# A graph network on one core: SP fetches seven tiles by rows instead of five, with their indices read five at a time, and the two padding tiles are not gathered

## What is computed

```python
edge_index = jnp.stack([src, dst])
h = jnp.maximum(_layernorm(x, axis=-1), 0.0)
x = x + _L0_gnn_ref(h, src, dst, L0_gnn_weight, L0_gnn_b)             # mean of h[src] (and self), times W
h = jnp.maximum(_layernorm(x, axis=-1), 0.0)
x = x + _L1_gnn_ref(h, W1, W2, b1, b2, edge_weight, src, dst)         # sum of weight * h[src], two products, a norm
h = jnp.maximum(_layernorm(x, axis=-1), 0.0)
x = x + _L2_gnn_ref(h, edge_attr_128, ..., src, dst)                  # sum of hn[src] * edge_net(edge_attr)
h = jnp.maximum(_layernorm(x, axis=-1), 0.0)
x = x + _L3_gnn_ref(h, edge_index, W, att_src, att_dst, bias, ...)    # softmax over the edges of a node, 4 heads
```

## Time and profile before

| | |
|---|---|
| median of the three executions shown | 4206.68 us |
| the profiled execution's own time | 4208.87 us |
| its span, first to last instruction | 4207.6 us |
| POOL busy | 3014.1 us (72%), of it the gathers of L675 2943.5 us |
| DVE busy | 2599.9 us (62%) |
| PE busy, its weight loads | 2442.4 us (58%), 2042.1 us (49%) |
| ACT busy | 1818.6 us (43%) |
| gathers on POOL | 3116 |

### The profile page before, as it was taken

One profiled execution on the slowest core, in us unless ns is written; L12 is line 12 of the kernel. 1 busy time (PEld: TensorE's weight loads), 2 busy tenths in 40 slices (PEclk: granted clock), 3 DMA queues, 4 the chain that ended last, 5 costly groups with the idle time before them and its releaser, 6 DMA issues.

```text
span 4207.6 us, 67388 instructions
## 1 busy us (share of the span) xinstructions
PE 2442.4 (58%) x13316; PEld 2042.1 (49%) x13316; DVE 2599.9 (62%) x7231; ACT 1818.6 (43%) x4182; POOL 3014.1 (72%) x3188
## 2 busy tenths in 40 slices
PE   2666666655556666666444444444656666666667
PEld 1455455554445555555444334444545554554556
DVE  4444444443566666667544444344559999999998
ACT  3444444421344444432211111112447887877875
POOL 3777777777677777777477777777747777777764
PEclk8778888776687888877656666666768999889988
DMA  4444444432344344432233333333456222222221
GB/s 132 110 124 118 121 124 116 122 90 66 88 121 124 114 124 118 121 104 68 78 104 107 105 109 104 109 109 109 115 106 119 57 57 57 57 57 58 57 47 31
DMA packets 238975, 405.80 MB, mean 96 GB/s; under 512 B 66706, under 2 KB 137515, under 8 KB 238572
## 3 DMA queue, kind: packets, MB, share of 16 engines
q0 software_dynamic: 99968, 207.33, 20.4%
q10 hardware_dynamic: 78736, 125.09, 10.5%
q1 hardware_dynamic: 59868, 69.07, 5.3%
HBM read 332.15 MB, written 67.78 MB: 95 GB/s over the span
## 4 chain that ended last, share of the span: by engine, by line
POOL 48%; issue 27%; SPq 10%; DMA 7%; DVE 4%; PE 2%; ACT 2%; ACTq 0%; DVEq 0%; POOLq 0%
POOL t_work L675 48%; DMA t_work<-d_T,t_tabG 6%; SPq L636 6%; SPq L702 4%; ACT t_acc L306 0%; PE ps L1914 0%; DVE t_acc L1883 0%; DVE ps L1371 0%; DVE t_x L1946 0%; DVE t_x L986 0%; PE ps L1337 0%; DVE t_halves L837 0%; DVE t_dev L299 0%; DMA t_tabG<-in_wgt 0%; ACTq L224 0%
## 5 line engine op out<-in xcount | busy, mean ns | idle before, releaser
L675 POOL DMA_INDIRECT t_work<-d_T,t_tabG x3116 | 2943.5, 945 | 1072.6 <-issue 922.3
L1337 PE MATMUL ps<-t_work,t_acc 128*128 x2592 | 450.1, 333 | 445.4 <-SPq L734 424.4
L1337 PEld LDWEIGHTS ps<-t_work,t_acc 128*128 128x128 f32 x2592 | 401.2, 238 | 518.7 <-issue 518.2
L1398 DVE TENSOR_TENSOR t_acc<-t_acc,ps 128x128 f32 (+1 forms) x732 | 210.6, 288 | 668.3 <-PE ps L559 342.7
L1387 DVE TENSOR_TENSOR t_hT<-t_work,ps 128x512 f32<-128x512 f32 x244 | 167.3, 686 | 510.8 <-ACT ps L1474 510.6
L1474 ACT COPY ps<-t_acc 128x512 f32 x244 | 140.5, 588 | 788.7 <-SPq L734 781.5
L1337 PE MATMUL ps<-t_hT,t_acc 128*128 128x128 f32 x1296 | 268.6, 392 | 289.6 <-DVE t_acc L1398 285.4
L1337 PEld LDWEIGHTS ps<-t_hT,t_acc 128*128 128x128 f32 x1296 | 252.5, 298 | 307.7 <-DVE t_hT L1387 301.8
L592 ACT ACTIVATE t_acc<-ps,t_bcol 128x1024 f32<-128x1024 f32 x98 | 109.1, 1113 | 660.0 <-DVE ps L605 654.1
L1774 PE MATMUL ps<-t_work,t_hT 128*128 x1960 | 324.0, 315 | 92.7 <-DVE t_acc L1784 77.6
L1337 PE MATMUL ps<-t_work 128*128 x1312 | 235.5, 342 | 243.6 <-SPq L734 221.0
(11 more groups left out here) (189 smaller groups left out, 4413.5 us busy)
## 6 DMA issues: line engine op xcount, KB each, us to landing
d_edge_net<-t_acc ACTq DMA_DIRECT2D x98, 512.0 KB
t_acc<-d_edge_net SPq DMA_DIRECT2D x98, 512.0 KB, 4.0
t_work<-d_T,t_tabG POOLq DMA_INDIRECT x3116
t_acc<-in_edge_attrT ACTq DMA_DIRECT2D x96, 512.0 KB, 4.2
t_acc<-d_T SPq DMA_DIRECT2D x1280, 0.5 KB
t_acc<-d_T SPq DMA_DIRECT2D x640, 0.5 KB
t_work<-d_T SPq DMA_DIRECT2D x640, 0.5 KB
t_acc<-d_T ACTq DMA_DIRECT2D x12, 790.1 KB, 15.6
```

What stands on the lines that cost most here:

```text
L675: pool.indirect_dma_start(out=work[:, at:at + width], out_offset=None, in_=table, in_offset=bass.IndirectOffsetOnAxis(ap=idx[:, g * QUAD + ...
L1337: last = pe.matmul(sums(layer, s, width), masks[s % MASKS][:, k, :], rows_k, start=(k == 0), stop=(k == QUAD - 1))
L1398: dve.tensor_tensor(out=o, in0=o, in1=sums(layer, s, width), op=ALU.add).then_inc(e_acc[layer], 1)
```

## The change

`SIDE` goes from 5 to 7 tiles and `SIDE_PER` from 4 to 5 rows per group. The side tiles now belong to groups 36, 62, 87, 113, 138, 164 and 190. Their 896 source indices are put in order by the host as one row, `sides`, in DRAM. SP brings them into SBUF 64 at a time, in two buffers (`read_sources`), and reads up to five of them into registers with one load, instead of one load per row out of the index table. Padding tiles 782 and 783 are not gathered any more (`gathers_of`), so group 195 has two gathers; nothing is added up from these two places in either kernel.

```diff
-SIDE, SIDE_PER = 5, 4
+SIDE, SIDE_PER, SIDE_READ = 7, 5, 64
...
+SIDE_READS = SIDE * P // SIDE_READ
...
+        def gathers_of(g):
+
+            return min(QUAD, ET - QUAD * g) - (g in SIDE_AT)
+
...
-                for k in range(QUAD - (g in SIDE_AT)):
+                for k in range(gathers_of(g)):
...
+        s_src = [sem(f"s_src{k}") for k in range(2)]
+
...
+        def side_sources(layer, c):
+
+            row = acc[0:1, NT * ACC3:XC] if layer < 3 else work[0:1, (RING * QUAD + 2) * ROW3:]
+            return row[:, c % 2 * SIDE_READ:(c % 2 + 1) * SIDE_READ].bitcast(I32)
+
...
+        def read_sources(layer, c):
+
+            sp.dma_start(side_sources(layer, c), a["sides"][0:1, c * SIDE_READ:(c + 1) * SIDE_READ])\
+                .then_inc(s_src[c % 2], 16)
 
         def fetch_rows(layer, table, n):
 
             width = table.shape[1]
-            for j in range(SIDE):
-                at = QUAD * SIDE_AT[j] + QUAD - 1
-                for p in range(max(SIDE_PER * (n - SIDE_BEGIN[j]), 0), min(SIDE_PER * (n + 1 - SIDE_BEGIN[j]), P)):
-                    row, = numbers(ENG.SP, idx[p:p + 1, at:at + 1], 1, 0, N - 1)
+            for c in range(SIDE_READS):
+                lo, hi = [min(max(SIDE_PER * m - SIDE_READ * c, 0), SIDE_READ) for m in (n, n + 1)]
+                if lo == hi:
+                    continue
+                if lo == 0:
+                    sp.wait_ge(s_src[c % 2], 16 * (SIDE_READS // 2 * layer + c // 2 + 1))
+                found = numbers(ENG.SP, side_sources(layer, c)[:, lo:hi], hi - lo, 0, N - 1)
+                for r, row in zip(range(c * SIDE_READ + lo, c * SIDE_READ + hi), found):
+                    j, p = divmod(r, P)
                     sp.dma_start(side_rows(layer, j)[p:p + 1, 0:width], table[bass.ds(row, 1), :])\
                         .then_inc(s_row[layer][j % 4], 16)
+                if hi == SIDE_READ and c + 2 < SIDE_READS:
+                    read_sources(layer, c + 2)
...
-            return sum(16 * (QUAD - (m in SIDE_AT)) for m in range(n % RING, n + 1, RING))
+            return sum(16 * gathers_of(m) for m in range(n % RING, n + 1, RING))
...
+            for c in range(2):
+                read_sources(layer, c)
...
+        "sides": np.concatenate([src[QUAD * g + QUAD - 1] for g in SIDE_AT]).reshape(1, SIDE * P),
```

More of the change, by code:

```diff
@@ L40 @@
 assert STEPS % 2 == 0
+SIDE_READS = SIDE * P // SIDE_READ
+assert P % SIDE_READ == 0
 assert SIDE_AT[-1] < GROUPS
@@ L691, in side_rows @@
             return (acc if layer < 3 else work[:, RING * QUAD * ROW3:])[:, lo + j % 2 * width:lo + (j % 2 + 1) * width]
-        assert MLP + 11 * GRP + 2 * ACC3 <= BB * ACC3 and (RING * QUAD + 2) * ROW3 <= work.shape[1]
+        def side_sources(layer, c):
+            row = acc[0:1, NT * ACC3:XC] if layer < 3 else work[0:1, (RING * QUAD + 2) * ROW3:]
+            return row[:, c % 2 * SIDE_READ:(c % 2 + 1) * SIDE_READ].bitcast(I32)
+        assert MLP + 11 * GRP + 2 * ACC3 <= BB * ACC3 and NT * ACC3 + 2 * SIDE_READ <= XC
+        assert (RING * QUAD + 2) * ROW3 + 2 * SIDE_READ <= work.shape[1] and SIDE_READS % 2 == 0
+        def read_sources(layer, c):
+            sp.dma_start(side_sources(layer, c), a["sides"][0:1, c * SIDE_READ:(c + 1) * SIDE_READ])\
+                .then_inc(s_src[c % 2], 16)
         def fetch_rows(layer, table, n):
             width = table.shape[1]
-            for j in range(SIDE):
-                at = QUAD * SIDE_AT[j] + QUAD - 1
-                for p in range(max(SIDE_PER * (n - SIDE_BEGIN[j]), 0), min(SIDE_PER * (n + 1 - SIDE_BEGIN[j]), P)):
-                    row, = numbers(ENG.SP, idx[p:p + 1, at:at + 1], 1, 0, N - 1)
+            for c in range(SIDE_READS):
[7 more added lines that the diff above has]
+                    j, p = divmod(r, P)
                     sp.dma_start(side_rows(layer, j)[p:p + 1, 0:width], table[bass.ds(row, 1), :])\
                         .then_inc(s_row[layer][j % 4], 16)
+                if hi == SIDE_READ and c + 2 < SIDE_READS:
+                    read_sources(layer, c + 2)
         def place_rows(layer, table, pitch, j):
```

## The result

The changed kernel took 4191.17 us (median of 6 runs, 4189.44 to 4193.27) against 4206.85 us for the kernel before (6 runs, 4204.90 to 4209.48). The ratio is 0.9961, with a 95% interval of 0.9952 to 0.9971: 15.7 us less, where 20.1 were forecast. It is faster by more than the 0.2% that a measurement can tell, it lies inside the range, 4.6 us above the 4186.6 us of the likeliest case and within 0.2 us of the 4191.0 us of the rival "layer 3 gives less".

The account below looks back on a forecast made before the run. POOL's gathers were taken to bound every layer, with the node stage ending layer 1. Gains of 5.0 + 1.25 + 5.0 + 4.3 + 4.6 = 20.1 us gave 4186.6 us, range 4181.5 to 4195.5.

Parts of the forecast that it names:

- layer 3 gives less: Rival: in layer 3, landings set the start's rounds or DVE follows POOL too closely; about 4191.0 us; chance 0.16.
- three signs of being wrong: POOL waits for SP mid-layer, a consumer takes over in layer 2 before the last gather, or a five-value load exceeds 1 us.
- Layer 0, 5.0 us: Layer 0, ended by POOL: four gathers fewer, all gained, 5.0 us against 11.37 us that DVE has to spare.
- Layer 2, 5.0 us: Layer 2, ended by POOL: four gathers fewer, all just gained, 5.0 us against 5.15 us of DVE idle time.
- in step: Rival: consumers already keep step with POOL, so layers 2 and 3 gain little; 4199.7 us; chance 0.08.
- Layer 1, 1.25 us: Layer 1, ended by the node stage: only one gather fewer ahead of gather 683 counts, 1.25 us gained.
- gated by POOL after all: Rival: POOL ends layer 1, so all four gathers count there, 3.75 us more gain; 4182.8 us; chance 0.12.
- Layer 3, tiles 2.5 us and padding 1.76 us: Layer 3: two side tiles gain 2.5 us; padding gains 1.76 us, limited by DVE's spare time; together 4.3 us.
- Start of layer 3, 4.6 us: Start of layer 3: SP's shorter fetch saves 1.15 us in each of four rounds, adding up to 4.6 us.
- The load of five, 0.5 us: SP's row fetches: one load of five index values takes 0.5 us, with ends of 0.45 and 0.6.
- SP becomes the bound, 4367 us: Rival: a load of five costs like five loads, so SP holds POOL back in all layers; 4367 us; chance 0.02.
- Small transfers one after the other: Rival: row DMAs pay their fixed time in sequence, 10 us per group, at least 1880 us per layer; chance 0.01.

Follow-up runs that it names:

- k0: The kernel before, plus one register operation per wait for a computed count, raising that count to at least 1; 4206.48 us.
- k1: The changed kernel with the same added register operation per wait as k0; 4191.75 us, ratio 0.9961 to the kernel before.
- k6: k5's form with eleven side tiles and eight rows per group, read by aligned loads of eight, instead of seven tiles and five rows; 4171.20 us.
- k7: k5's form with ten side tiles and seven rows per group, read by aligned loads of seven, instead of seven tiles and five rows; 4182.47 us.
- k2: k0 with only the gathers of the two padding tiles left out; five side tiles and one load per row stay; 4199.43 us.
- k5: k1 with each group's indices laid out eight words apart, so every load of five starts at a multiple of 16 bytes; 4192.47 us.
- k4: k0 with four indices read by one 16-byte-aligned load instead of one load per row; five side tiles and gathered padding stay; 4205.27 us.
- k3: k1 with each row's index read by its own load, as before the change, instead of five per load; 4561.44 us, ratio 1.0839.
- k8: k6's form with twelve side tiles and nine rows per group; 5881.10 us, ratio 1.0911, on a chip where the kernel before took 5389.02 us.
- k11: The same kernel as k8 on another chip, where the kernel before took 5381.98 us; 5878.49 us, ratio 1.0925.

## Why the prediction was right, and where it was not

The time came inside the range, but as the rival "layer 3 gives less" (0.16) has it and not as the likeliest case (0.60): the four counts of gathers held, and the 4.6 us at layer 3's start did not. Two of the prediction's three signs of being wrong were seen, a load of five over 1 us and a consumer on the chain in layer 2 before the last gather; neither cost what they were taken to announce, since SP and the consumers still had time to spare. The third, POOL waiting for SP in the middle of a layer, was not: in layer 0 the 68 waits that SP ends sum to 20.7 us, 0.304 each, the usual pause.

- **Layer 0, 5.0 us.** Right: 5.3 in both pairs, the profiled one and k0 with k1. POOL ends this layer.
- **Layer 2, 5.0 us.** 4.0 in the profiled pair and 7.1 in k0 with k1. POOL's part is exact (4.9 us from first to last gather); the node stage behind it varies by more than the difference. The rival "in step" has some truth: the chain passes through DVE and PE now. But k6 still gained 10.9 us here, for eight gathers fewer, so the consumers had not become the bound.
- **Layer 1, 1.25 us.** The gate moved by 1.29 us as forecast, and k6 and k7 gained 6.6 and 2.9 us by the same count of side tiles before group 171. The idle time of POOL after the layer's last gather grew by 4.3 us in the profiled pair and by 3.2 from k0 to k1, where 3.75 was forecast. The layer's own gain of 1.25 us is too small to be seen in one pair (-0.1 and 1.6 us). The rival "gated by POOL after all" fell: by it k6 and k7 would have gained 10.0 and 8.7 us there, and leaving out the padding gained nothing in k2, once its slower pace is allowed for.
- **Layer 3, tiles 2.5 us and padding 1.76 us.** The layer is 6.9 us shorter in the profiled pair and 6.6 from k0 to k1. Less what its start gave (2.5 and 1.0 us), that is 4.4 and 5.6, against 4.3. And in the changed kernel DVE has no idle time over 0.25 us left after the last gather, where it had 1.76 us before: it took over at the end as forecast.
- **Start of layer 3, 4.6 us.** This is the step that failed. The start gave 2.5 us in the profiled pair and 1.0 from k0 to k1, so it makes up 2.1 to 3.6 of the 4.4 us between forecast and result; the rest is no larger than the difference between two executions. The prediction said "With the change the SP part shrinks from 4.1 to 2.95 us" and "each round starts from the one before, so the gains add up". The first was near (3.29 us measured for a group's fetch), with k5 at the assumed price. The second was wrong: SP's fetch stood on the chain, but right beside it stood landings of 7 to 9 us and slots not yet read, and they took over within a few groups. k4 cut the fetch by 1.65 us per group and gained nothing that shows; its chain of waits runs through ACT, DVE and PE there, and SP waits 12.7 us for PE. The prediction had weighed DVE's idle time after 3215 us (37.4 us) and not before it: in these first 112 us DVE waits for landed groups only 3.5 us in the kernel before. The reading of the chain was right for what it is, one path, and did not tell how close the next one lay.
- **The load of five, 0.5 us.** Wrong: 0.69 to 1.23 us, outside the range of 0.45 to 0.6. It cost nothing that shows, since SP's 204 us of waiting in layer 2 covered it, and since the one place that depended on it gave nothing that shows at any price. The row of four `closing` numbers at 0.466 us misled, being as cheap as k4's aligned loads of four (0.462); DVE's load of eight at 0.597 us did too.
- **SP becomes the bound, 4367 us.** Its mechanism was real and its size too small. k3 is the case described there, five loads for five rows, and took 4561 us with the padding's gain included, some 0.5 us per group in layer 0 where 0.1 was reckoned. The sum of medians left out the tail of the loads (0.12 us per group, by the mean of 0.533) and more of the rest of a group.
- **Small transfers one after the other.** Fell: k6 issues 2048 small fetches more than the changed kernel and is 20 us faster. The Trainium skill, "DMA: Bandwidth & Descriptors", Rules for kernel authors, advises to coalesce small transfers, since under 64 KB one mostly pays overhead. By that advice taken alone k6 should have been slower. The overhead is there, 0.41 us of SP for every 0.5 KB row, but it is paid on an engine that had the time.

The account by the measured parts: padding 7.05 us (k0 to k2), tiles with their reading 7.7 us (k2 to k1), 14.7 together for k1, and 15.7 for the changed kernel. By the pace, without the start of layer 3, the forecast was 6.8 + 8.75 = 15.5.

## What to carry to other kernels

Where an engine is the bound by its number of instructions at a fixed pace, count the instructions, find for each stage the gate that ends it, and count only those ahead of the gate; that gave every term here that held. A piece of work on the chain of waits is worth its time only until the next path, so before pricing its removal look at what else arrives just before (the landings, and the last reader of the buffer), and at whether the consumers wait at all in that stretch. A chain that changes its path from one execution to the next means two paths of one length. And moving work to a helper queue pays until that queue's waiting time is used up; read that time as a budget, stage by stage (in layer 2 167.7 us before, 204.0, then 10.5 in k6), with the tail of its instructions counted and not their median alone.

## What the runs showed of the hardware that was not expected

- What a load of several values into SP's registers costs depends on its address. Medians: one value 0.44 to 0.52 us, four from a multiple of 16 bytes 0.46 (k4), four from elsewhere 0.88 (changed kernel), five from a multiple of 16 bytes 0.68 to 0.69 (k5), five from elsewhere 1.07 to 1.23, eight aligned ones 0.69 (k6), nine 0.91 (k8). Seven aligned ones cost 1.09 (k7), more than eight. For these aligned loads 0.46 us for the first four words, and 0.22 for each further four or each single word left over, comes close (1.12 for the seven); it is a fit to five numbers and no more.
- The issue of a one-row DMA on SP took 0.225 us in the median where the indices were loaded together, and 0.255 us where a load stood before each (k3). Why was not tried.
- Two executions can differ by over 2 us in a node stage that neither version touches (layer 2's ends 48.0 us after the last gather in the changed kernel's profile, 45.6 in k1's). A difference of a microsecond between two profiles is no evidence by itself.
- On two of the chips SP executed stretches of its stream at about 0.7 us per instruction, register operations included (k8 to k11), and the kernel before took 5389 and 5382 us there instead of 4207. POOL kept its pace of 1.249 us where SP did not hold it up.
